# Neighbour rows stored by SyncE amid the clearing of the count table, and counts scattered four, then five, six and seven groups behind the gathers

## What is computed

```python
# part 1: messages along edges, then dense layers on the nodes
g   = einsum('pr,fr->pf', edge_attr_16, W_att)          # a filter for each edge
x_j = ssp(einsum('nf,gf->ng', ssp(x), W_j) + b_j)       # "neighbour rows"
m   = x_i + segment_sum(x_j[dst] * g, src)              # pairs are (src, dst)
...                                                     # three residual layers, W_v, layernorm
# part 2: two attention layers, two heads of 64
alpha = einsum('ehc,ehc->eh', q[dst], k[src]) / 8
amax  = segment_max(alpha, dst)
ex    = exp(alpha - amax[dst]); denom = segment_sum(ex, dst)
out   = segment_sum(ex / denom[dst] * v[src], dst).mean(heads)
```

## Time and profile before

| | |
|---|---|
| median of 3 runs | 3566.74 us |
| the runs | 3565.88 to 3567.86 us |
| the profiled execution | 3568.79 us, of which 3567.0 us are the span of the profile |
| mean granted clock of TensorE | 0.956 of full speed |
| start of the first scatter | 156.37 us |
| start of the last scatter | 2401.00 us |
| first load of counts (SP L415) | 2410.19 us |
| first L1120 of DVE | 2440.46 us |

### The profile page before, as it was taken

One profiled execution on the slowest core, in us unless ns is written; L12 is line 12 of the kernel. 1 busy time (PEld: TensorE's weight loads), 2 busy tenths in 40 slices (PEclk: granted clock), 3 DMA queues, 4 the chain that ended last, 5 costly groups with the idle time before them and its releaser, 6 DMA issues.

```text
span 3567.0 us, 64347 instructions
## 1 busy us (share of the span) xinstructions
PE 3189.7 (89%) x20040; PEld 1823.8 (51%) x20040; DVE 2898.0 (81%) x8886; ACT 999.1 (28%) x1689; POOL 2667.4 (75%) x1764
## 2 busy tenths in 40 slices
PE   4989999999999999999999999976788888899996
PEld 2666666666666666666666666642222222322222
DVE  5788888888888888888888888868677775877886
ACT  3111111111111111111111111133455554233433
POOL 2288888888888888888888888861787888476874
PEclk6999999999999999999999999987899999999998
DMA  8733333333333333333333333315544452332320
GB/s 277 280 50 48 44 47 49 50 49 49 50 46 43 49 50 50 49 50 46 43 49 50 49 49 49 39 2 148 150 132 146 132 151 72 80 89 76 89 64 9
DMA packets 265753, 271.38 MB, mean 76 GB/s; under 512 B 145252, under 2 KB 224717, under 8 KB 265673
## 3 DMA queue, kind: packets, MB, share of 16 engines
q1 hardware_dynamic: 87751, 162.29, 15.3%
q0 software_dynamic: 131712, 19.76, 13.0%
q10 hardware_dynamic: 46210, 88.29, 8.2%
HBM read 189.11 MB, written 81.07 MB: 76 GB/s over the span
## 4 chain that ended last, share of the span: by engine, by line
POOL 47%; PE 19%; issue 16%; DMA 6%; DVE 6%; ACT 3%; SPq 2%; POOLq 1%; DVEq 0%; ACTq 0%
POOL edge_counts L476 27%; POOL nodes_and_gaps L467 14%; PE PS L1396 6%; PE PS L1419 6%; DMA edge_counts<-small 4%; POOL scores L531 4%; PE PS L1428 3%; SPq L395 2%; POOL counts_and_logs L514 1%; DVE scores L1134 1%; DVE PS L1145 1%; DVE counts_and_logs L1120 1%; PE PS L1408 1%; DMA edge_counts<-counts_and_logs 1%; ACT scores L721 1%
## 5 line engine op out<-in xcount | busy, mean ns | idle before, releaser
L1295 PE MATMUL PS<-scores 128*128 128x320 bf16 x11760 | 1707.5, 303 | 127.0 <-DVE scores L966 70.5
L1295 PEld LDWEIGHTS PS<-scores 128*128 128x128 bf16 x11760 | 1156.1, 99 | 660.1 <-DVE scores L966 153.0
L476 POOL DMA_INDIRECT edge_counts<-small x752 | 1213.1, 1613 | 275.4 <-issue 275.4
L531 POOL TENSOR_TENSOR scores<-scores,max_of_targets 125x896 f32<-125x896 f32 x335 | 701.8, 2143 | 191.2 <-ACT max_of_targets L716 141.8
L467 POOL DMA_INDIRECT nodes_and_gaps<-xj_rows,small x588 | 582.5, 991 | 248.6 <-issue 161.3
L966 DVE TENSOR_SCALAR scores<-scores,small 128x192 bf16<-128x192 bf16 x3136 | 748.1, 304 | 3.4
L881 DVE SCALAR_TENSOR_TENSOR scores<-scores,small,PS 128x512 bf16<-128x512 f32 x784 | 573.0, 731 | 0.0
L1134 DVE TENSOR_TENSOR scores<-PS,counts_and_logs 125x896 f32<-125x896 f32 x350 | 377.8, 1082 | 203.9 <-PE PS L1396 76.6
L616 ACT ACTIVATE scores<-nodes_and_gaps 128x512 bf16<-128x512 f32 x98 | 61.7, 630 | 1392.4 <-DVE nodes_and_gaps L944 848.0
L721 ACT ACTIVATE scores<-scores 125x896 f32<-125x896 f32 x350 | 329.8, 948 | 372.9 <-POOL scores L531 366.0
L1396 PE MATMUL PS<-q_features,k_features 64*125 64x448 f32 x1400 | 371.1, 612 | 67.9 <-DVE scores L1134 65.0
(11 more groups left out here) (192 smaller groups left out, 2125.0 us busy)
## 6 DMA issues: line engine op xcount, KB each, us to landing
counts_and_logs<-edge_counts SPq DMA_DIRECT2D x70, 980.0 KB
scores<-tile_keys ACTq DMA_DIRECT2D x96, 512.0 KB
edge_counts<-counts_and_logs SPq DMA_DIRECT2D x50, 766.0 KB
edge_counts<-counts_and_logs SPq DMA_DIRECT2D x35, 980.0 KB
running_max<-fetch_targets ACTq DMA_DIRECT2D x48, 312.5 KB
max_of_targets<-fetch_targets ACTq DMA_DIRECT2D x48, 312.5 KB
edge_counts<-small POOLq DMA_INDIRECT x752
nodes_and_gaps<-xj_rows,small POOLq DMA_INDIRECT x588
```

The costliest lines, as they stand in the source:

```text
L476: pool.indirect_dma_start(cnt_dram, bass.IndirectOffsetOnAxis(ap=index[:, s:s + 1], axis=0), value[:, s:s + 1], None, compute_op=ALU.add). ...
L531: nc.gpsimd.tensor_tensor(t, t, MB, ALU.subtract).then_inc(sem("shifted"), 1)
L1295: ins = nc.tensor.matmul(PS[:, b, 0:HI * F], onehot[:, s, b * P:b * P + 128], spread[:, s, i].rearrange("p h f -> p (h f)"), start=first a ...
```

## The change

*SP and ACT.* SP issues three fills before it waits for the padded edges, and two after the first features. The weights, key and target stores follow, then three more fills. Then SP waits for ACT's four copies of the neighbour rows (`xj_part`) and stores the rows itself; ACT doesn't store them any more. Then it waits for the stores of keys and targets, loads those of groups 0 and 1, and issues the other 42 fills without a further wait.

*POOL and DVE.* At the groups 26, 50 and 74 (`STEPS` 13, 25, 37, in pairs of groups) POOL gathers and doesn't scatter, and from then on its scatters are one group further behind: five, six and seven. The hardware loops of POOL and DVE are split in four at these places, with two groups written out ahead of each part. DVE stages the counts for the new distance and none at the groups 24, 48 and 72. Seven groups, 56 scatters, remain behind the loop.

```diff
--- before.py
+++ after.py
@@ -51,8 +51,9 @@
 assert SLOTS == NT + LEAD and EARLY + 7 == JPP == NT - 4 and NT + JLEAD == EARLY
 assert ND >= N and D <= 512 and MW <= P
 FILLS = 50
+FIRST_FILLS = 3
+SECOND_FILLS = 5
 EARLY_FILLS = 8
-FIRST_FILLS = 3
 ROUND = 4
 FILL = -(-(N * ND + ROUND * EP) // (128 * FILLS))
 FETCHED = (G // 2 - 1, G - 1)
@@ -64,6 +65,10 @@
 PIECES = 3
 VHI = HI - 1
 BEHIND = 4
+STEPS = (13, 25, 37)
+STARTS = (BEHIND // 2,) + STEPS
+ENDS = STEPS + (NG // 2,)
+LATEST = BEHIND + len(STEPS)
 EARLIER = 2 * ROUND * EP
 SPLIT = P // 16 * 16
 BIG = 1e30
@@ -360,39 +365,48 @@
 
         @block.sync
         def _(sp):
+            def clear(a):
+
+                sp.dma_start(cnt_fills[:, a, :], cfill).then_inc(sem("counts_cleared"), 16)
+
             xv = x.rearrange("(t p) f -> p t f", p=P)
             for q in (slice(0, SPLIT), slice(SPLIT, P)):
                 sp.dma_start(X[q, :, 0, :], xv[q, 0:HALF, :]).then_inc(sem("x_loaded"), 16)
                 sp.dma_start(X[q, 0:NT - HALF, 1, :], xv[q, HALF:NT, :]).then_inc(sem("x_loaded"), 16)
             load_weights(sp, 0)
+            sp.dma_start(Watt, W_att).then_inc(sem("watt_loaded"), 16)
+            sp.wait_ge(sem("fills_set"), 1)
+            for a in range(FIRST_FILLS):
+                clear(a)
             sp.wait_ge(sem("edges_padded"), 2)
             for a, dest in ((src, src_i), (dst, dst_i)):
                 for q, width, keys in edge_parts(a):
                     sp.dma_start(dest[q, 0:width], keys.rearrange("(p j) -> p j", p=q.stop - q.start)
                                  ).then_inc(sem("edges_loaded"), 16)
-            sp.dma_start(Watt, W_att).then_inc(sem("watt_loaded"), 16)
             for u in range(2):
                 load_features(sp, u, u)
 
-            sp.wait_ge(sem("fills_set"), 1)
-            for a in range(FILLS):
-                if a == FIRST_FILLS:
-                    sp.wait_ge(sem("wblk_zeroed"), 1)
-                    sp.wait_ge(sem("wattT_copied"), 1)
-                    for j in range(G):
-                        sp.dma_start(Wblk[R * j:R * j + R, F * j:F * j + F], WattT).then_inc(sem("wblk_ready"), 16)
-                    sp.wait_ge(sem("keys_out"), 2)
-                    sp.dma_start(key_dram.rearrange("(j p) e -> p j e", p=KB), key_turned).then_inc(sem("rows_stored"), 16)
-                    sp.wait_ge(sem("targets_cut"), 5)
-                    sp.dma_start(target_dram.rearrange("g (c e) -> g c e", e=EP), target_cut.rearrange("p f c e -> p (f c) e")).then_inc(sem("rows_stored"), 16)
-                    sp.wait_ge(sem("rows_stored"), 32)
-                    for u in range(2):
-                        load_keys(sp, u, u)
-                        load_targets(sp, u, u)
-                if a == EARLY_FILLS:
-
-                    sp.wait_ge(sem("xj_stored"), 32)
-                sp.dma_start(cnt_fills[:, a, :], cfill).then_inc(sem("counts_cleared"), 16)
+            for a in range(FIRST_FILLS, SECOND_FILLS):
+                clear(a)
+            sp.wait_ge(sem("wblk_zeroed"), 1)
+            sp.wait_ge(sem("wattT_copied"), 1)
+            for j in range(G):
+                sp.dma_start(Wblk[R * j:R * j + R, F * j:F * j + F], WattT).then_inc(sem("wblk_ready"), 16)
+            sp.wait_ge(sem("keys_out"), 2)
+            sp.dma_start(key_dram.rearrange("(j p) e -> p j e", p=KB), key_turned).then_inc(sem("rows_stored"), 16)
+            sp.wait_ge(sem("targets_cut"), 5)
+            sp.dma_start(target_dram.rearrange("g (c e) -> g c e", e=EP), target_cut.rearrange("p f c e -> p (f c) e")).then_inc(sem("rows_stored"), 16)
+            for a in range(SECOND_FILLS, EARLY_FILLS):
+                clear(a)
+            sp.wait_ge(sem("xj_part"), 4)
+            for q in (slice(0, SPLIT), slice(SPLIT, P)):
+                sp.dma_start(xj_dram.rearrange("(t p) f -> p t f", p=P)[q], XJn[q, 0:NT, :]).then_inc(sem("xj_stored"), 16)
+            sp.wait_ge(sem("rows_stored"), 32)
+            for u in range(2):
+                load_keys(sp, u, u)
+                load_targets(sp, u, u)
+            for a in range(EARLY_FILLS, FILLS):
+                clear(a)
             for l, (wq, bq, wk, bk, wv, bv, ws, bs) in enumerate(layers):
                 for w, dest in ((wq, wq_(l)), (wk, wk_(l)), (wv, wv_(l)), (ws, ws_(l))):
                     sp.dma_start(dest, w).then_inc(sem("layer_weights"), 16)
@@ -477,28 +491,31 @@
                                         value[:, s:s + 1], None, compute_op=ALU.add
                                         ).then_inc(sem("count_added"), 16)
 
-            def group(g, u, scatters):
+            def group(g, u, behind):
                 pool.wait_ge(sem("targets_staged"), g + 1)
-                if scatters:
-                    pool.wait_ge(sem("counts_staged"), 2 * (g - BEHIND) + 2)
+                if behind is not None:
+                    pool.wait_ge(sem("counts_staged"), 2 * (g - behind) + 2)
                 settled()
                 for s in range(0, G, ROUND):
-                    if scatters:
+                    if behind is not None:
                         for e in range(ROUND):
-                            scatter(g - BEHIND, s + e, cidx[u], cnt[u])
+                            scatter(g - behind, s + e, cidx[(u + behind) % 2], cnt[(u + behind) % 2])
                     for e in range(ROUND):
                         if s + e not in FETCHED:
                             gather(g, u, s + e)
 
             pool.wait_ge(sem("xj_stored"), 32)
             for g in range(BEHIND):
-                group(g, g % 2, False)
+                group(g, g % 2, None)
             pool.wait_ge(sem("counts_cleared"), 16 * FILLS)
-            with pool.Fori(BEHIND // 2, NG // 2) as k:
-                for u in range(2):
-                    group(2 * k + u, u, True)
+            for j, (first, end) in enumerate(zip(STARTS, ENDS)):
+                group(2 * first, 0, None if j else BEHIND)
+                group(2 * first + 1, 1, BEHIND + j)
+                with pool.Fori(first + 1, end) as k:
+                    for u in range(2):
+                        group(2 * k + u, u, BEHIND + j)
             pool.wait_ge(sem("indexed"), 2 * NG)
-            for h in range(NG - BEHIND, NG):
+            for h in range(NG - LATEST, NG):
                 for s in range(G):
                     scatter(h, s, cidx_all[:, h * G:(h + 1) * G], cnt_all[:, h * G:(h + 1) * G])
 
@@ -593,8 +610,6 @@
                                      ACT.Copy).then_inc(sem("xj_part"), 1)
                 nc.scalar.activation(XJn[:, HALF * h + 12, :], PS[0:P, 3, F * h:F * h + F], ACT.Copy).then_inc(sem("xj_part"), 1)
             act.wait_ge(sem("xj_part"), 4)
-            for q in (slice(0, SPLIT), slice(SPLIT, P)):
-                act.dma_start(xj_dram.rearrange("(t p) f -> p t f", p=P)[q], XJn[q, 0:NT, :]).then_inc(sem("xj_stored"), 16)
 
             def copy_fT(g):
                 act.wait_ge(sem("fT_in_psum"), g + 1)
@@ -862,9 +877,9 @@
 
                 nc.vector.tensor_copy(dcur[u], dst_i[:, bass.ds(g * G, G)]).then_inc(sem("targets_staged"), 1)
 
-            def stage_counts(h, u, first):
-
-                if not first:
+            def stage_counts(h, u):
+
+                if not isinstance(h, int) or h > 1:
                     dve.wait_ge(sem("count_added"), 16 * G * (h - 1))
                 nc.vector.tensor_copy(cidx[u], cidx_all[:, bass.ds(h * G, G)]).then_inc(sem("counts_staged"), 1)
                 nc.vector.tensor_copy(cnt[u], cnt_all[:, bass.ds(h * G, G)]).then_inc(sem("counts_staged"), 1)
@@ -931,7 +946,7 @@
                     dve.wait_ge(sem("tile_summed"), G * (g - 1) + s + 1)
                 nc.vector.tensor_scalar(onehot[:, s, :], iota_h, los[:, s:s + 1], None, ALU.is_equal).then_inc(sem("low_matched"), 1)
 
-            def compute(g, u, k, first, counts, last, end):
+            def compute(g, u, k, first, behind, last, end):
                 sl = bass.ds(g * G, G)
                 if not isinstance(g, int) or g:
                     dve.wait_ge(sem("last_fifth_spread"), G * g)
@@ -944,8 +959,8 @@
                 nc.vector.tensor_tensor(msg, gx[u], PS[:, 6, :], ALU.mult).then_inc(sem("messages"), 1)
                 if not last:
                     stage_targets(g + 2, u)
-                if counts is not None:
-                    stage_counts(g + 2 - BEHIND, u, counts)
+                if behind is not None:
+                    stage_counts(g + 2 - behind, (u + behind) % 2)
                 dve.wait_ge(sem("rows_staged"), 2 * g + 2)
                 for s in range(2):
                     match_low(g, s, first)
@@ -1016,18 +1031,21 @@
                 for h in range(HI):
                     take_fifth(0, f, h, 0)
 
-            def edge_group(g, u, k, first=False, counts=None, last=False, end=False):
+            def edge_group(g, u, k, behind, last=False, end=False):
                 if not end:
                     stage_keys(g + 1)
```

(19 more changed lines are left out.)

## The result

The changed kernel takes 3607.49 us (median of 4 runs, 3604.47 to 3613.5) against 3567.3 us: a ratio of 1.0112, interval 1.0097 to 1.0127, some 40 us slower. The forecast was 3556 and the range ended at 3590; the time lies outside it, on the side of the locked rival. The profiled execution took 3606.07 us, 37.3 more than that of before. By the bound of the prediction this is slower.

What follows compares the result with a forecast made beforehand. The path through edge loop and dense layers, held to POOL's pace, sets the end. Counts +56.8 tail, −46.1 gathers, −4 start, +1.5 loops put L1120 13.0 earlier; 2 for clock and logarithm: 3566.74 − 11.0, say 3556; range 3545 to 3590.

Steps and rivals of the forecast that it cites:

- the locked rival: Edge loop: DVE stays in step with POOL's pattern, leaving lead unused; 3582 us, 3600 if none is taken up; chance 0.33.
- the bound of the prediction: Whole kernel: faster is under 3559.6 us, slower over 3573.9; chances faster 0.50, slower 0.37, same 0.13.
- The tail: Behind the edge loop: 24 moved scatters add 6 rounds of 9.47 us each, +56.8 us.
- Slack of the counts: Before L1120: the counts could come 21.1 us later before they, not edge loop and dense layers, set the end.
- The start: Clearing stage: fills 9 to 50 no longer wait for the neighbour rows' landing; gain 4 us, bounds −2 and 10.
- The loops: POOL and DVE leaving one hardware loop and entering another: 0.5 us each time, 1.5 in all, bounds 0 and 3.
- The wait of 17.4 us: Clearing stage: SyncE stood 17.4 us at L395 for the neighbour rows' store; later fills started near 55.7.
- Does the pace follow?: Edge loop: DVE and PE must take up 15.4 us within 24 groups, at 1.68 us a group.
- the edge path: Path through edge loop and dense layers to L1120: 46.1 us earlier, from 15.4 us of POOL saved three times.
- The break-even pace: Edge loop: 22.55 us a group, at which 11 us of the 46.1 are lost.
- half a pattern: Edge loop: halves of POOL's pattern are 11.5 us long; only lead that exceeds a half is taken up.
- for which I had 2: Around L1120: PE's first scores at half speed and a logarithm no longer done ahead, 2 us, bounds 0 and 4.

Runs made afterwards that it cites:

- one step: Kernel before, with POOL leaving out a group's scatters only at group 26, old start, 40 scatters in the tail: 3572.37 us, ratio 1.0019.
- the steps alone: Kernel before with the change's POOL and DVE parts (groups 26, 50, 74 without scatters) but the old start: 3609.87 us, ratio 1.0123.
- two half steps: Kernel before, with POOL leaving out one round of four scatters at group 26 and another at 50, old start: 3569.52 us, ratio 0.9998.
- mixed with one step: Kernel before, no scatters at group 26, each round two scatters, one gather, two scatters, two gathers: 3570.89 us, ratio 1.0011.
- mixed with the change: The whole change, with each round as two scatters, one gather, two scatters, two gathers: 3593.03 us, ratio 1.0067 against the kernel before.
- start with half step: Kernel before with the change's SP and ACT parts, and one round of four scatters left out at group 26: 3558.69 us, ratio 0.9976.
- POOL's copies: Scatters of the first 94 groups replaced by POOL copying an SBUF tile onto itself, 1.5 to 1.7 us each: 4225.43 us, one execution.

## Why the prediction was wrong

**What held.** The change's parts and their places were right. Six gathers take POOL 7.5 us, where I had 7.7. The tail: six rounds forecast at 56.8, measured 57.8. Slack of the counts 21.1: with one step and 19 us more of tail L1131, the line of L1120, starts at 2434.3, just the 6.2 us earlier that the last message is. The time rose by 0.19% (0.06 to 0.32) all the same, by a loss further on that is told below. The start: 2.4 us at the first scatter for my 4, below that in the time; the same sign, within the bounds. The loops: nothing. (The wait of 17.4 us began at 38.3: from the 38.78 that I named, the sum would be 56.2 and not 55.7. Nothing hangs on it.)

**What failed** is the step "Does the pace follow?". It took 21.41 us a group for the pace that PE and DVE have when POOL is early. That row is one group written out ahead of the loop, with no POOL beside it. In the loop the pace is 22.43 without scatters, and 23.09 with them whatever the lead. Of the 46.1 us that I put on the edge path, two arrived (7.0 less the 4.8 of the start). The break-even pace that I had worked out, 22.55, shows how little the forecast could bear: with the right row for the free pace it would have stood on the edge.

**The rival that came true** is the locked pace. Its place was right to 0.1 us: half a pattern, 11.4, of lead stays (15.2 − 3.8). It was priced at 3582, at 3600 if nothing is taken up; measured are 3607. Three terms were missing. The counts' path: 57.8 for the rounds, less 5.8 (tail's first scatter 2323.32 against 2329.16), less 21.1, and 10.9 us from load to L1138 where I had 9.1: +32.7, and 32.6 measured. At each step a hold that I had no row for: behind nine gathers in a row DVE waits 8.8, 7.8 and 7.9 us for the fetched rows. Of the second, timelines of PE and DVE:

```profile
1211.52 0.44 PE L1313 MATMUL PS<-scores 128*128 128x320 bf16 x2 [0.98 <-issue]
```

```profile
1214.50 0.28 DVE L938 TENSOR_SCALAR nodes_and_gaps<-PS,small 128x64 f32<-128x64 f32 x1 [7.82 <-remote]
```

PE had ended these rows at 1206.76, and the update of their semaphore is at 1214.40, 7.64 us later. Meanwhile PE runs its next matmuls in ones and twos, with 0.3 to 1.1 us between them in which it waits for nothing that the profile shows. The message behind it comes 31.1, 28.1 and 28.1 us after the one before, in place of 23.1.

And 4.7 us are lost behind L1138 in the profiled execution (37.3 − 32.6), for which I had 2. Windows of the kernel before and of the changed one, around the same matmuls between the two attention layers:

```profile
2984.90:3005.40 20.50, 20.50 (x70) 5.72 (x70) 3.42 (x5) 8.10 (x12) 20.50 (x11) 0.84 0.00 1
```

```profile
3014.80:3035.30 20.50, 20.20 (x45) 5.39 (x46) 2.55 (x4) 5.56 (x8) 20.50 (x11) 0.50 0.00 0
```

PE is granted 1.2 GHz for 6.8 us in the first and for 20.5 in the second; there the distance to the kernel before grows from 29.9 to 37.8 us. The profiled executions of the steps alone, one step, two half steps, mixed with one step, mixed with the change, and start with half step have the same 20.5 us; those of the others that scatter in the loop have 6.8. It costs one step the gain of its 6.2 us, and it makes differences of up to 8 us between two profiled executions say little about the edge loop. What decides between 6.8 and 20.5 us isn't shown.

**Chances.** The views that spoke for the rival were read (DVE hardly waits for gathers and is yet no faster than POOL; a wait of L923 ends with the second scatter of a round), and were then given 0.33. They were worth more than a pace from one group.

**Still open** is how a scatter holds the message. That the wait ends with the second of four scatters in a row is shown, that what comes late is the update of a semaphore of PE, and that the lead is taken up when a gather stands between; why the update is late isn't. It isn't a matter of scatters alone: without any in the loop the semaphore of the transposed features (L1270, L1265 there), for which ACT waits, is 0.7 to 3.1 us late beside the six gathers in each of 78 groups, and no wait ahead of a message comes of it. Open also is why PE itself slows down beside nine gathers, and why the second half step's lead went up.

## What to carry to other kernels

Before work is moved off a busy engine so that another may catch up, measure that other one's pace in the very loop, beside the same neighbours, with the work left out; one group ahead of a loop is no measure. When an engine keeps exactly another's pace without waiting for its data, look for what its waits end with: here those for the fetched rows and for the filters ended with a scatter, and the order of four scatters and three gathers decided whether 15 us of lead were used or kept. And work moved from a place where its wait is covered to a tail where it is bare should be priced against slack first: 57 us against 21 could pay only if nearly all of the gain arrived.

## What the runs showed of the hardware

Beside four scatters in a row the update of a PE semaphore comes up to 2.3 us behind the end of its matmul, with the end of the second scatter. It held DVE's message 1.4 us, 17 times in 81 groups, though its gathers had landed, and its fetched rows in 64 of them. Beside nine gathers in a row it came 7.6 us late. Beside POOL's copies the same two semaphores were never late.

A copy on POOL beside DVE: 690 to 1806 ns for a product of two SBUF tiles, 304 to 440 for the bf16 scaling, 731 and 731 with one input in PSUM. The Trainium skill, "SBUF — State Buffer", section "Who interferes with whom", says just this: an instruction with two SBUF inputs contends with a GpSimd instruction that reads SBUF, one in a two-port mode contends with GpSimd, and one with at most one SBUF input outside these modes does not. This run agrees for the two products; whether the scaling was in such a mode no run shows. The scatters' hold is not that rule's: the product stays at 690 beside them, and the held message has one input in PSUM. The prediction gave the rule without this condition, and by the condition it would not have tied L944 to the scatters.

A stop of PE of 2.06 us was followed by 3.4 us at 1.2 GHz, and so were 15 others of 2.02 to 2.10; the mean granted clock of the loop is 1.00 without scatters and 0.98 with them.

The small steps ahead of a message took 0.62 us written out and 1.05 or 1.67 in the loop, with the same instructions.
